# A fused recurrent-attention and expert kernel: normalisation added in pairs, and row weights picked by GpSimd

## The reference

```python
xn = _layernorm(x)
x  = x + attn(xn, ...) + ffn(xn, ...)
# attn: a recurrence in logarithms
k = xn @ W_z.T + b_z
log_h = cumsum(-softplus(k), features) + cumlogsumexp(values - that, time)
log_h = (log_h - log_h.mean()) / std(log_h)      # over everything
y = exp(log_h) + xn
attn = (y - mean) * rsqrt(var + eps) * ln_w + ln_b      # per row
# ffn: the best 2 of 8 experts for each of the 2048 rows
ffn = sum over experts e of  w_e * (silu(xn @ w1[e].T) * (xn @ w3[e].T)) @ w2[e].T
```

## Time and profile before

| What | us |
|---|---|
| median of 3 runs (357.09 to 359.14) | 357.22 |
| the profiled execution, its own time | 357.79 |
| its span, first to last instruction | 356.1 |
| TensorE matmul busy | 325.8 (91%) |
| VectorE busy | 260.8 (73%) |
| ScalarE busy | 219.9 (62%) |
| GpSimd busy | 206.4 (58%) |

### The profile page before, as it was taken

One profiled execution on the slowest core, in us unless ns is written; L12 is line 12 of the kernel. 1 busy time (PEld: TensorE's weight loads), 2 busy tenths in 40 slices (PEclk: granted clock), 3 DMA queues, 4 the chain that ended last, 5 costly groups with the idle time before them and its releaser, 6 DMA issues.

```text
span 356.1 us, 6682 instructions
## 1 busy us (share of the span) xinstructions
PE 325.8 (91%) x1964; PEld 273.9 (77%) x1964; DVE 260.8 (73%) x466; ACT 219.9 (62%) x328; POOL 206.4 (58%) x137
## 2 busy tenths in 40 slices
PE   8998999799999999999898999999999999979830
PEld 8883464588878898997787899889898988969730
DVE  5488787989996899889899842584589668763300
ACT  2547997455879974999854269934853485323400
POOL 4500023159968674989899728563885475945331
PEclk9999969989999999999999999999999999999985
DMA  7924912005444542354354434542463534354621
GB/s 263 426 120 137 293 52 59 15 11 150 122 82 115 142 101 32 80 129 129 44 144 109 102 38 115 142 101 33 84 181 89 75 45 76 47 76 49 98 38 15
DMA packets 19086, 37.00 MB, mean 104 GB/s; under 512 B 2272, under 2 KB 13536, under 8 KB 19008
## 3 DMA queue, kind: packets, MB, share of 16 engines
q0 software_dynamic: 9168, 11.97, 21.5%
q1 hardware_dynamic: 8496, 22.56, 20.4%
q10 hardware_dynamic: 1376, 1.85, 1.4%
HBM read 27.45 MB, written 11.03 MB: 108 GB/s over the span
## 4 chain that ended last, share of the span: by engine, by line
PE 54%; DVE 23%; ACT 8%; issue 8%; DMA 2%; ACTq 1%; POOL 1%; POOLq 0%; DVEq 0%
PE PS L1296 23%; PE PS L1314 11%; PE PS L1190 6%; PE PS L1326 5%; DVE wrow L1067 3%; DVE tmp L961 3%; PE PS L1176 2%; DMA out<-work,sidx 2%; DVE hT L956 2%; DVE U L985 2%; DVE A L998 1%; PE PS L1220 1%; DVE xrow L1054 1%; DVE xrow L1059 1%; PE PS L1265 1%
## 5 line engine op out<-in xcount | busy, mean ns | idle before, releaser
L1296 PE MATMUL PS<-wbuf,xT 128*128 128x512 f32 (+1 forms) x648 | 149.6, 384 | 4.9 <-issue 3.7
L1296 PEld LDWEIGHTS PS<-wbuf,xT 128*128 128x128 f32 x648 | 118.3, 190 | 29.4 <-issue 9.3
L424 POOL TENSOR_TENSOR wbuf<-raw,wbuf x28 | 81.4, 2924 | 23.1 <-ACT wbuf L604 21.4
L406 POOL DMA_INDIRECT out<-work,sidx x35 | 62.7, 1792 | 53.2 <-ACT work L621 20.1
L1314 PE MATMUL PS<-wbuf,hT 128*128 128x256 f32 x648 | 86.8, 288 | 0.0
L1314 PEld LDWEIGHTS PS<-wbuf,hT 128*128 128x128 f32 x648 | 79.3, 189 | 1.9 <-issue 1.9
L390 POOL DMA_INDIRECT work<-xn_dram,gidx x39 | 50.4, 1292 | 51.8 <-DVE gidx L892 36.1
L595 ACT ACTIVATE tmp<-PS 128x512 f32<-128x512 f32 x72 | 32.0, 460 | 41.6 <-PE PS L1296 41.3
L961 DVE TENSOR_TENSOR tmp<-tmp,PS 128x512 f32<-128x512 f32 x72 | 35.0, 516 | 29.4 <-ACT tmp L595 28.6
L956 DVE TENSOR_TENSOR hT<-PS,hT 128x768 fp32r<-128x768 f32 x36 | 34.2, 949 | 29.3 <-ACT hT L590 24.2
L621 ACT ACTIVATE work<-PS,wrow 128x256 f32<-128x256 f32 x35 | 16.4, 470 | 38.0 <-PE PS L1314 38.0
(11 more groups left out here) (185 smaller groups left out, 350.7 us busy)
## 6 DMA issues: line engine op xcount, KB each, us to landing
raw<-w_main SPq DMA_DIRECT2D x24, 544.0 KB
raw<-w_main SPq DMA_DIRECT2D x8, 416.0 KB
xn_dram<-xrow SPq DMA_DIRECT2D x4, 516.0 KB, 7.2
out<-xrow POOLq DMA_DIRECT2D x4, 512.0 KB, 6.1
xrow<-x SPq DMA_DIRECT2D x4, 256.0 KB, 4.8
xrow<-x ACTq DMA_DIRECT2D x4, 256.0 KB, 5.4
small_sb<-small ACTq DMA_DIRECT2D x1, 768.0 KB, 7.9
work<-xn_dram,gidx POOLq DMA_INDIRECT x39
```

Source lines behind the costliest of these rows:

```text
L406: pool.indirect_dma_start(out, bass.IndirectOffsetOnAxis(sidx[:, j:j + 1], 0), ysb[:, j % DEEP, :], None, compute_op=ALU.add).then_inc(s_s ...
L424: pool.tensor_tensor(lo, raw[:, ds(part, WP)], hi.bitcast(fp32), ALU.subtract).then_inc(s_w, 1)
L1296: ins = pe.matmul(PS[:, at:at + cols], xT[:, slot, xpart, q * P:(q + 1) * P], wbuf[:, w, wpart, q * 2 * F + at:q * 2 * F + at + cols], sta ...
```

## The change

Four things are changed.

1. `slot_weight` moves from VectorE to GpSimd, as a tensor_scalar with two operations on 128 x 1 elements. GpSimd does it for tile j+2 at the head of its tile j; for tiles 0, 1 and 2 it is done before the loop, around `gather(4)`.
2. `row_deviations` goes from tiles 24 and 28 to tiles 23 and 27 on ScalarE (with the table loads around it). On VectorE `row_scales` goes from tiles 25 and 29 to 24 and 28, and `last_norm(0)` to `last_norm(5)` go to tiles 24 to 29, one tile sooner; `last_norm(6)` stands in `between(30)` and `last_norm(7)` in `after(30)`, where they were in tiles 31 and 32.
3. `add_attention` adds two pieces at a time, ahead of tiles 28 and 31, and nothing behind the loop.
4. The 12 small matmuls ahead of the last `down` are gone.

```diff
-LAST_FILL = 12
...
+            def slot_weight(j):
+
+                k = j % DEEP
+                pool.wait_ge(s_gt[k], 16 * (j // DEEP + 1))
+                pool.tensor_scalar(wrow[:, j:j + 1], xg[:, k, D:D + 1], first_pick[:, j:j + 1],
+                                   xg[:, k, D + 1:D + 2], ALU.mult, ALU.max).then_inc(s_ws, 1)
...
-            def add_attention(j, m):
-
-                pool.wait_ge(s_p2, 4 * m + 4)
-                rows_added(j, m)
-                pool.dma_start(out[4 * m * P:4 * (m + 1) * P, :].rearrange("(t p) d -> p t d", p=P),
-                               xn[:, 4 * m:4 * m + 4, :], accum_op=ALU.add).then_inc(s_ab, 16)
+            def add_attention(j, first):
+
+                pool.wait_ge(s_p2, 4 * first + 8)
+                rows_added(j, first)
+                for m in (first, first + 1):
+                    pool.dma_start(out[4 * m * P:4 * (m + 1) * P, :].rearrange("(t p) d -> p t d", p=P),
+                                   xn[:, 4 * m:4 * m + 4, :], accum_op=ALU.add).then_inc(s_ab, 16)
...
-            for j in range(DEEP + 1):
+            for j in range(DEEP):
                 gather(j)
             pool.wait_ge(s_idx, 1)
+            slot_weight(0)
+            gather(DEEP)
+            slot_weight(1)
+            slot_weight(2)
             pool.wait_ge(s_ctl, 1)
...
+                if j + 2 < NTILES:
+                    slot_weight(j + 2)
                 if j + DEEP < NTILES:
                     gather(j + DEEP)
                 scatter(j - 1, parts)
...
-                    if j in (27, 29, 31):
+                    if j in (28, 31):
                         add_attention(j - 1, added)
-                        added += 1
+                        added += 2
                     done = tile(i, u, done, added)
-            add_attention(SURE - 1, added)
...
-                    row_deviations((j - 24) // 4)
+                    row_deviations((j - 23) // 4)
...
-                    elif j in (18, 24, 28):
+                    elif j in (18, 23, 27):
...
-                dve.scalar_tensor_tensor(wrow[:, j:j + 1], xg[:, k, D:D + 1], first_pick[:, j:j + 1],
-                                         xg[:, k, D + 1:D + 2], ALU.mult, ALU.max).then_inc(s_ws, 1)
...
+                if j == 30:
+                    last_norm(6)
...
-                if j in (25, 29):
-                    row_scales((j - 25) // 4)
-                if 25 <= j <= 32:
-                    last_norm(j - 25)
+                if j in (24, 28):
+                    row_scales((j - 24) // 4)
+                if 24 <= j <= 29:
+                    last_norm(j - 24)
+                if j == 30:
+                    last_norm(7)
...
-                    slot_weight(j + 1)
...
-                warm(LAST_FILL)
```

More of the change, by code:

```diff
@@ L1061, in last_norm @@
                 ins.then_inc(s_p2, 1)
-            def slot_weight(j):
-                k = j % DEEP
-                dve.wait_ge(s_gt[k], 16 * (j // DEEP + 1))
-                dve.scalar_tensor_tensor(wrow[:, j:j + 1], xg[:, k, D:D + 1], first_pick[:, j:j + 1],
-                                         xg[:, k, D + 1:D + 2], ALU.mult, ALU.max).then_inc(s_ws, 1)
             softplus(0)
@@ L1076, in _ @@
             x_lo(0, 0, xT0_ps)
-            slot_weight(0)
             softplus(2)
@@ L1080, in _ @@
             x_lo(1, 1, xT1_ps)
-            slot_weight(1)
             dve.wait_ge(s_u0b, 2)
```

## The result

The changed kernel takes **363.49 us**, the median of 4 runs (362.3 to 363.92). The kernel before takes 357.22. The ratio is 1.016, with a 95% interval from 1.0131 to 1.0189: **1.6% slower**. The prediction was 351.4, with a range from 347.0 to 355.8, and it was wrong in its sign. The execution profiled took 363.92, its span was 362.2, and 1.7 lay around it as before.

The account below looks back on a forecast made before the run. GpSimd's chain of additions bounds the end, TensorE with pauses the part before. Gains of 3.3 us up to tile 27 and 2.5 in the chain cut the span from 356.1 to 350.3: time 351.4 against 357.22, range 347.0 to 355.8.

Parts of the forecast that it names:

- The row weight on GpSimd: GpSimd's row-weight pick takes 0.3 us, between 0.1 and 1.0; covered mid-kernel by four buffers, hidden in the final chain.
- The stall of VectorE in tiles 12 to 17: VectorE's row-weight stalls there: moving the row weight off gains 2.0 of the 7.4 us lost, between 0 and 4.5.
- R2: Stalls only move to the next SBUF instruction: 0.8 instead of 3.3 us up to tile 27; time 353.9, chance 0.16.
- Tile 26: Without the row-weight stall at 260.89, the normalisation avoids a subtraction and TensorE's transposes come about 0.8 us earlier.
- The table loads: Table-load pair on ScalarE goes to tiles 23 and 27: may delay the next silu, -0.3 us (0 to -1.7).
- Part 2: Last normalisation one tile sooner: gain booked at zero, from +1.3 to -3, on TensorE with slack behind it at the end.
- R5: Nothing much: row-weight gains given back in tiles 29 to 31 by a late TensorE; 355 to 358, chance 0.07.
- Part 3: Attention pairs in GpSimd's addition chain: a pair takes 10.5 us, last scatter at 345.3 instead of 347.79, 2.5 us gained.
- R1: The two additions of a pair run side by side: 8.1 instead of 10.5 us each pair; time 348.4, chance 0.19.
- R4: Paired additions hinder each other: at 15.3 us a pair the kernel is 3.8 us slower, 361.0; chance 0.03.
- Part 4: Small matmuls dropped before the last down: result copied 0.66 us sooner, hidden behind the additions, worth nothing.
- The case of the fall: If the clock fell, the last down's 2.4 us would double, result at 344.3, still hidden before the scatter at 345.3.

Follow-up runs that it names:

- Part 1 alone: Kernel before with only the row weights moved to GpSimd, two tiles ahead: 363.44 us, ratio 1.0198.
- the idle reading operation: Kernel before, VectorE's row weight with one SBUF tensor, plus a GpSimd tensor_scalar whose result nobody reads: 361.91 us, ratio 1.0159.
- the kernel with the one-tensor row weight: Kernel before with VectorE's row weight as a tensor_scalar, one SBUF tensor and two per-partition scalars: 356.25 us, ratio 0.999.
- the kernel with PSUM: Changed kernel, row weight on VectorE with one SBUF tensor, last four normalisation row pairs reading weight and bias from PSUM: 352.53 us, ratio 0.990.

## Why the prediction was wrong

The sum was -3.3 up to tile 27 and -2.5 in the chain of additions. Measured, on the same ruler, +6.5 at tile 18, +7.25 at tile 27, and the end bound by another engine.

- **The row weight on GpSimd: the step that failed.** "I take 0.3", between 0.1 and 1.0, and "mid-kernel four buffers cover it". It measured 1454 ns in the mean; 0.35 to 0.4 where free, 3.03 at most. The mean of 1.0 was no upper bound: it came from VectorE, and on GpSimd the same lock holds it from the other side, against scans of 2.28 us. The cover was the wrong one as well. Four buffers hide a late gather; they do not stop a late subtraction or scatter from meeting VectorE's scans. GpSimd had no time left there either (23.6 us busy of 25). The prediction had both halves ("the pick, now itself GpSimd's, can wait for one of VectorE's scans and hold up the gather and scatter behind it") and gave the second no price in tiles 12 to 16. Part 1 alone cost 6.7 us (363.44 less 356.74), and the idle reading operation, which moves nothing, 5.7.
- **The stall of VectorE in tiles 12 to 17.** Booked as 2.0 gained of 7.4. They took 209.57 - 156.64 = 52.9 us where they took 48.6: 4.3 lost. The 2.0 rested on "VectorE would win some races"; it lost more of them, since GpSimd's scatter and subtraction come without a gap between them. The rival R2, that stalls only move, was right as a mechanism: the kernel with the one-tensor row weight shows it by itself. Even a row weight that is never held was worth nothing in the median and in tiles 12 to 17 (48.7), so the 2.0 was no gain to be had here. In the changed kernel two falls of the clock lie in these tiles too; the sum had no term for them.
- **Tiles 7 and 8** lost 1.7 us that no term had. They are the same meetings, in the second expert: two sums of VectorE at 129.34 took 4.65 us where they took 2.35, beside the subtraction of 128.66.
- **The small terms.** Lead-in, booked 0.3: `up(0)` at 63.47 in both. Tile 3, booked 0.5: it took 7.4 us instead of 7.1. Tile 26, where the stall of 260.89 was to give 0.8: with part 1 alone it took 7.97 instead of 8.09, and in the changed kernel 8.88. There the normalisation, one tile sooner now, met another subtraction: two instructions at 272.15 took 4.30 us beside the one of 273.06. The table loads, booked -0.3 in tile 23: 7.28 in both.
- **Part 2** was booked at zero, "from +1.3 to -3", and alone it is zero (1.0011). "Behind which there is slack at the end" was the fault: with the pairs it cost TensorE 9 us where the row weight stayed on VectorE, and 4.6 in the changed kernel, and the slack was 5.2. Net of what tile 32 gave back it is 3.2 from `up(26)` to `up(35)`, about what part 1 alone lost there. The prediction moved the quarters to 293 to 299.6 in its own working and had the normalisation in tiles 29 and 30 there too, but priced their meeting as one stall of before (R5, chance 0.07).
- **Part 3** was right in its terms. Pair 10.5: measured 10.7 and 10.95, 10.4 in the kernel with PSUM, and 9.7 to 10.95 over all kernels with pairs. So R1 (8.1) and R4 (15.3) fell. Steps of the scatters 4.7: measured 4.0 to 4.2. From the last scatter's start to the end 8.3: 8.3. Freed of the stalls, the kernel with PSUM started its last scatter at 341.95, 5.8 sooner than before, and took 352.53. That both are near the forecast (5.8 and 351.4) is luck: the 3.3 of the front was not there, 1.6 lie ahead of tile 0, and from `up(26)` to the last scatter it gained 4.1, not 2.5.
- **Part 4** was hidden only while the additions set the end. Its 0.66 for the start of the last `down` was not there in the changed kernel's profile: it came 3.1 us behind the end of the transposes, before 3.0. In the five other kernels without the fill it came 2.2 to 2.6 behind, in the other seven with it 2.7 to 3.7, so the term is there in most of them. The clock then cost 0.8 in the open. The case of the fall had been worked out (2.4 us more) and called hidden.

Which signs were named and seen: `wrow` above 0.4 us, the stalls found again on the scans (R2's sign), a last scatter released by ScalarE (half of R1's sign, without its pair of 8 us), and the last line of the prediction, that the loss in tiles 12 to 17 grows. The chances have a slip: the forecast, R1 and a third of R2 make 0.71 at most, not 0.74.

## What to carry to other kernels

An instruction moved from VectorE to GpSimd to get out of a stall between the two stays in it if it reads SBUF; here it was then held by VectorE's long work and shifted later meetings. Take the operand away instead: a per-partition scalar or a copy of a constant in PSUM leaves one SBUF tensor, and the instruction runs in its free time beside GpSimd. That is worth something only where no other two-tensor instruction takes the stall over: for the row weight it gave nothing (356.25 us), for the last normalisation 7.4 us (359.97 to 352.53). A step that holds a queue (here a pair of additions of 10.5 us) must be priced with what stands behind it in that queue and whom that then meets; slack of an engine is spent once, so add up all the steps that are booked on it.

## What the runs showed of the hardware

- VectorE's tensor_scalar of 128x1, one SBUF tensor and two per-partition scalars from SBUF: 255 to 270 ns in every one of eight profiles, whatever GpSimd did beside it. scalar_tensor_tensor with two SBUF tensors: 0.2 to 3.8 us.
- GpSimd's tensor_scalar of 128x1: 0.35 to 0.4 us free, 0.8 to 0.95 behind the issue of a scatter, up to 3.0 behind a scan. A memset of the same size: 0.09 to 0.8 us and no effect on the time that could be measured.
- VectorE did not get in between two of GpSimd's instructions that stood close: 6.08 us for a pair of 0.87, across two subtractions.
- Even the issue of an indirect DMA on GpSimd is held by a scan: 3.01 instead of 1.58 us in the kernel before.
- Two additions by DMA of 512 KB each behind one wait take 9.7 to 10.95 us to the scatter behind them (16 pairs), one 6.6 to 7.9 (24 of them): the second adds about 3.5 us, more than its issue of 1.4.
